# Other slots for a tail's events, a last tail in halves, and transfers asked for a stage sooner

## The reference

```python
theta = 2*pi*freq[ids]*t + phase[ids]
h = concat(amp[ids]*sin(theta), amp[ids]*cos(theta)) @ W_proj + b_proj + bias[ids]
x = layernorm(h)
Q, K, V = split(x @ W.T + b, 16 heads of 32)
S = K Q.T * scale + decay, causal           # softmax over S, times V
h = h + (softmax(S) @ V) @ o_w.T + o_b
x = layernorm(h)
score = sqrt(softplus(x @ gate_w.T))        # 32 experts
top6 of score + bias; weight = score / sum(score of top6) * 1.5
routed = sum over top6 (at most 192 rows an expert, in the order of the rows):
         weight * (silu(x @ w_gate) * (x @ w_up)) @ w_down
shared = clip(silu(x @ sg.T) * (x @ su.T), -10, 10) @ sd.T
out = h + routed + shared
```

## Time and profile before

| | before |
|---|---|
| median of 3 runs | 3718.28 us (3714.33 to 3722.51) |
| the profiled execution, its time | 3716.85 us |
| its span | 3715.1 us |
| TensorE busy, mean granted clock | 3207.5 us (86%), 0.935 |
| VectorE, ScalarE, GpSimd busy | 2157.7, 1201.6, 1756.5 us |
| embed, to | 261 us |
| attend, steps | 305 to 3224 us |
| last tail | 3224 to 3386 us |
| experts | 3386 to 3715 us |

### The profile page before, as it was taken

One profiled execution on the slowest core, in us unless ns is written; L12 is line 12 of the kernel. 1 busy time (PEld: TensorE's weight loads), 2 busy tenths in 40 slices (PEclk: granted clock), 3 DMA queues, 4 the chain that ended last, 5 costly groups with the idle time before them and its releaser, 6 DMA issues. The chain is left out here.

```text
span 3715.1 us, 61950 instructions
## 1 busy us (share of the span) xinstructions
PE 3207.5 (86%) x20352; PEld 1660.1 (45%) x20360; DVE 2157.7 (58%) x6046; ACT 1201.6 (32%) x2745; POOL 1756.5 (47%) x988
## 2 busy tenths in 40 slices
PE   4657999999899989999999898999999998675998
PEld 2333444444444444444444444444444443344775
DVE  6843444566656665666566656665666566663554
ACT  3651333233323332333333333333333333211111
POOL 5730454555555555555455545554555455622333
PEclk8878999999999999999999999999999998787999
DMA  5762300121111001100110011001100100005996
GB/s 189 254 258 84 100 30 12 35 74 57 59 59 50 23 24 36 37 22 22 38 35 23 21 39 35 22 23 38 35 21 25 37 15 21 29 15 166 258 257 151
DMA packets 121805, 253.61 MB, mean 68 GB/s; under 512 B 38748, under 2 KB 39388, under 8 KB 118928
## 3 DMA queue, kind: packets, MB, share of 16 engines
q1 hardware_dynamic: 76720, 197.22, 16.0%
q0 software_dynamic: 44048, 49.26, 5.2%
q10 hardware_dynamic: 720, 3.15, 0.2%
HBM read 144.61 MB, written 202.16 MB: 93 GB/s over the span
## 5 line engine op out<-in xcount | busy, mean ns | idle before, releaser
L855 POOL TENSOR_TENSOR a_first_probs<-a_first_probs,a_probs 128x2048 f32<-128x2048 f32 (+3 forms) x320 | 1030.6, 3221 | 1130.5 <-ACT a_probs L941 1038.7
L1084 DVE CUSTOM_DVE_ANT_0 a_unused<-a_ps_ring,a_decay 128x512 bf16<-128x512 f32 (+3 forms) x1536 | 778.6, 555 | 957.5 <-PE a_ps_ring L1374 952.0
L941 ACT ACTIVATE a_probs<-a_ps_ring 128x512 f32<-128x512 f32 (+3 forms) x1280 | 505.0, 472 | 461.1 <-PE a_ps_ring L1408 286.8
L1398 PE MATMUL a_ps_ring<-a_k_t,a_q_t 32*128 32x512 f32 (+3 forms) x3072 | 412.0, 538 | 66.6 <-DVE a_row_max L1084 44.4
L866 POOL DMA_INDIRECT d_slots<-a_rows,a_place_i x373 | 379.2, 1017 | 134.4 <-issue 71.6
L1374 PE MATMUL a_ps_ring<-a_q_t,a_k_t 32*128 32x512 f32 (+3 forms) x3072 | 396.5, 540 | 17.9 <-DVE a_row_max L1084 12.5
L1472 PE MATMUL a_ps_dense<-a_sd,a_inner_t 128*128 128x512 f32 x224 | 158.8, 848 | 147.4 <-DVE a_gate_up L1203 147.4
L941 ACT ACTIVATE a_first_probs<-a_ps_ring 128x512 f32<-128x512 f32 x256 | 135.7, 605 | 415.3 <-PE a_ps_ring L1408 392.3
L1398 PEld LDWEIGHTS a_ps_ring<-a_k_t,a_q_t 32*128 32x128 f32 x3072 | 144.8, 185 | 267.6 <-issue 147.9
L1421 PE MATMUL a_ps_heads<-a_probs,a_values 128*32 128x512 f32 (+3 forms) x2560 | 263.3, 484 | 0.0
L1362 PE MATMUL a_ps_dense<-a_normed_t,a_q_w 128*128 128x512 f32 x512 | 240.5, 613 | 24.7 <-DMA a_normed_t<-d_normed_t 22.2
(11 more groups left out here) (226 smaller groups left out, 4372.7 us busy)
## 6 DMA issues: line engine op xcount, KB each, us to landing
d_hidden<-e_hidden SPq DMA_DIRECT2D x8, 2048.0 KB
d_normed_t<-e_normed_t SPq DMA_DIRECT2D x8, 2048.0 KB
x_w_gate<-w_gate SPq DMA_DIRECT2D x32, 512.0 KB, 6.3
x_w_up<-w_up SPq DMA_DIRECT2D x32, 512.0 KB, 7.6
x_w_down<-w_down SPq DMA_DIRECT2D x32, 512.0 KB
a_normed_t<-d_normed_t SPq DMA_DIRECT2D x7, 2048.0 KB, 7.8
a_residual<-d_hidden SPq DMA_DIRECT2D x56, 256.0 KB, 2.7
d_hidden<-a_residual SPq DMA_DIRECT2D x56, 256.0 KB, 2.0
```

The source lines that it names most:

```text
L855: nc.gpsimd.tensor_tensor(total_of, total_of, probs_of(m)[:, :, 0:width], ALU.add).then_inc(added, 1)
L941: nc.scalar.activation(probs_of(m)[:, h, 0:width], score_bank(m, h)[:, 0:width], ACT.Exp).then_inc(exp_done, 1)
L1084: nc.vector.tensor_tensor_reduce(unused[:, (HG * k + h) % N_UNUSED, 0:width], row_bank(k, h)[:, 0:width], decay[:, at:at + width], 1.0, NE ...
L1398: nc.tensor.matmul(score_bank(m, h)[:, 0:width], q_t[st.g][dims, j * P:(j + 1) * P], k_t[st.g][dims, i0:i0 + width], start=True, stop=False)
```

## The change

1. **Slots.** Other entries in the tables.
2. **Last tail in halves.** Four tiles at once instead of two, in an order of 37 dense uses written out by hand, with six banks. `Part` holds the small tiles of a half, `late_parts` both; `find_late_places` is `find_places` for four tiles. Small operations on VectorE work on four tiles each; the shared expert still goes by quarters of two tiles (`late_inner`, `late_gate_up`). GpSimd multiplies the last heads ahead of the 12 scatters of the last step, and then issues 48.
3. **Shared tiles.** The q, k, v weights and the normed rows have tiles that live through all blocks (`Shared`). SP loads the weights in batch 2 of embed, and batch 0's rows between the stores of batch 6 and those of batch 7. The weights of experts 0 and 1 go to the same tiles (3 MB), issued by SP at the start of the last step, with the last batch's hidden rows; `load` leaves them out for these two. To make room, embed keeps its waves in the tile of its sines (so the sines of batch b wait until TensorE has turned the waves of b - 1), and some of its constants lie in the shared tiles.

```diff
-PROJECT_AT = {0: ((2, A), (3, A), (3, C), (4, C), (7, C), (9, C)),
-              1: ((0, C), (1, C), (2, C), (3, C), (7, C), (9, C)),
-              2: ((1, C), (2, C), (3, C), (4, C), (7, C), (9, C)),
-              3: ((0, C), (1, C), (2, C), (3, C), (7, C), (9, C))}
-OUT_AT = ((0, A), (0, C), (1, C), (2, C), (6, A), (7, A), (8, A), (9, A))
+PROJECT_AT = {0: ((2, C), (3, B), (3, C), (4, B), (7, C), (9, C)),
+              1: ((0, B), (1, C), (2, C), (3, C), (7, C), (9, C)),
+              2: ((1, C), (2, C), (3, C), (4, B), (7, C), (9, C)),
+              3: ((0, B), (1, C), (2, C), (3, C), (7, C), (9, C))}
+OUT_AT = ((0, A), (0, C), (1, C), (2, B), (6, B), (7, A), (8, A), (9, A))
-QUARTER_AT = {True: ((4, A), (4, B), (5, C), (6, C), (8, C), (10, C), (11, A), (11, C)),
-              False: ((4, A), (4, B), (5, C), (6, C), (8, C), (10, C), (11, A), (11, C))}
-STATS_AT = {True: (2, 1), False: (1, 1)}
-NORMALISE_AT = {True: (3, 1), False: (3, 1)}
-SOFT_SUM_AT = {True: (6, 1), False: (6, 1)}
+QUARTER_AT = {True: ((4, A), (4, C), (5, C), (6, C), (8, C), (11, A), (11, B), (11, C)),
+              False: ((4, A), (4, C), (5, C), (6, C), (8, C), (11, B), (11, B), (11, C))}
+STATS_AT = {True: (2, 1), False: (0, 1)}
+NORMALISE_AT = {True: (3, 1), False: (1, 1)}
+SOFT_SUM_AT = {True: (7, 1), False: (6, 1)}
-COUNT_AT = {True: (9, 1), False: (9, 1)}
+COUNT_AT = {True: (10, 0), False: (10, 0)}
-RSTD_AT = {True: 3, False: 2}
+RSTD_AT = {True: 3, False: 1}
-ROOT_AT = {True: 7, False: 7}
-LATE_SUMS_AT, LATE_MAXIMA_AT, EARLY_SUMS_AT, EARLY_MAXIMA_AT = (1, A), (1, B), (5, A), (5, B)
+ROOT_AT = {True: 7, False: 8}
+LATE_SUMS_AT, LATE_MAXIMA_AT, EARLY_SUMS_AT, EARLY_MAXIMA_AT = (1, A), (2, A), (5, A), (5, B)
-LATE_INVERT, EARLY_INVERT = (1, 2, 3, 4), (6, 8, 9, 10)
-LATE_MULTIPLY, EARLY_MULTIPLY = 5, 11
+LATE_INVERT, EARLY_INVERT = (1, 1, 4, 4), (6, 8, 8, 9)
+LATE_MULTIPLY, EARLY_MULTIPLY = 5, 10
-LATE_BANKS = 4
+LATE_BANKS = 6
+LATE = [("sums", 1, None), ("out", 1, None), ("out", 0, None), ("out", 2, None), ("out", 3, None),
+        ("out", 4, None), ("out", 5, None), ("turn", 0, None), ("turn", 1, None), ("turn", 3, None),
+        ("turn", 2, None), ("out", 6, None), ("route", 0, None), ("out", 7, None), ("up", 0, 0),
+        ("turn", 4, None), ("turn", 5, None), ("turn", 7, None), ("up", 1, 0), ("place", 0, None),
+        ("turn", 6, None), ("route", 1, None), ("up", 0, 2), ("up", 0, 1), ("up", 1, 1),
...
# embed, SP
+                if b == 2:
+                    sp.wait_ge(v_b_turned, 1)
+                    for tile, name, arrived in zip(common.projections, "qkv", common.weights_in):
+                        sp.dma_start(tile[:], io[f"{name}_w"]).then_inc(arrived, 16)
+                if b == NB - 2:
+                    sp.wait_ge(hidden_done, NT * (NB - 2))
+                    sp.wait_ge(normed_out[0], 16 * (NB // 2 - 1))
+                    first = common.normed_t()
+                    sp.dma_start(first[:, :, 0:HALF], dram["normed_t"][0, :, :, 0:HALF]).then_inc(common.normed_half_in, 16)
+                    sp.dma_start(first[:, :, HALF:T], dram["normed_t"][0, :, :, HALF:T]).then_inc(common.normed_in, 16)
...
# embed, ACT
-                wait_from_1(act, waves_done, b)
+                wait_from_1(act, wave_ps_full, 2 * b)
...
# attend, SP, at the start of the last step
+                if st.g == G - 1 and not st.rows:
+                    sp.wait_ge(scores_full, ITEMS * (FINAL - 2))
+                    for i in range(NT):
+                        sp.dma_start(late_hidden[i], dram["hidden"][NB - 1, tile_rows(i), :]).then_inc(late_in, 16)
+                    for e, (w_gate, w_up, w_down) in enumerate(common.weights()):
+                        sp.dma_start(w_gate, io["w_gate"][e]).then_inc(common.up_in[e], 16)
+                        sp.dma_start(w_up, io["w_up"][e]).then_inc(common.up_in[e], 16)
+                        sp.dma_start(w_down, io["w_down"][e]).then_inc(common.down_in[e], 16)
...
# VectorE, last tail
+            late_stats(7, chain)
+            take_moments(late_parts[1], chain)
+            normalise_late(1, chain)
+            choose(LATE_X + 0, late_parts[0], chain)
+            count_chosen(late_parts[0], chain)
+            find_late_places(0, late_parts[0], late("place", 0), chain)
+            late_gate(0, 0, chain)
+            soft_parts(late_parts[1], late("route", 1), chain)
+            soft_sum(LATE_X + 1, late_parts[1], chain)
...
# experts, load
+                if known is not None and known < FIRST_EXPERTS:
+                    return
```

More of the change, by code:

```diff
@@ L456 @@
 FINAL = G * NB
+LATE_X = QUARTERS * (NB - 1)
 SHIFT = 5
@@ L1121, in take_stats, with take_moments @@
+            def take_moments(k, chain):
                 chain.wait_apart(passed)
-                for j in range(2):
-                    chain.done(nc.vector.bn_aggr(moments[:, j, :], stats[:, j, :]))
+                for j in range(k.n):
+                    chain.done(nc.vector.bn_aggr(k.moments[:, j, :], k.stats[:, j, :]))
                 chain.wait()
-                nc.vector.tensor_scalar(variance[:], moments[:, :, 1], EPS, None, ALU.add).then_inc(var_done, 1)
-            def normalise(x, into, tiles, chain):
+                nc.vector.tensor_scalar(k.variance, k.moments[:, :, 1], EPS, None, ALU.add).then_inc(var_done, 1)
@@ L1220, in find_places @@
-                chain.done(nc.vector.tensor_tensor(place[:], place[:], over[:], ALU.add))
-                chain.done(nc.vector.tensor_tensor(counts_b[:], counts_b[:], chosen_b[:, 0, :], ALU.add))
+                chain.done(nc.vector.tensor_copy(rows[p][:, :, D], token[:]))
+                chain.done(nc.vector.tensor_tensor(k.place, k.place, k.over, ALU.add))
+                chain.done(nc.vector.tensor_tensor(counts_b[:], counts_b[:], k.chosen_b[:, 0, :], ALU.add))
                 chain.wait()
@@ L1336, in _ @@
             for_batches(dve, step)
-            for i in range(2):
-                add_late(i, late("out", i))
-            norm = norm_chain(0)
-            take_late_stats(0, norm)
-            for piece in range(PIECES):
-                invert_sums(1, piece, late("sums", 1))
-            normalise_late(0, norm)
-            for q in range(QUARTERS):
-                quarter(q)
+            chain = Chain(dve, late_step, 0)
+            add_late(1, late("out", 1))
+            add_late(0, late("out", 0))
@@ new lines, in _ @@
+            invert_sums(1, 0, late("sums", 1))
+            invert_sums(1, 1, late("sums", 1))
+            late_stats(1, chain)
+            invert_sums(1, 2, late("sums", 1))
+            add_late(2, late("out", 2))
+            invert_sums(1, 3, late("sums", 1))
+            late_stats(0, chain)
+            add_late(3, late("out", 3))
+            late_stats(3, chain)
+            late_stats(2, chain)
+            take_moments(late_parts[0], chain)
+            normalise_late(0, chain)
+            add_late(5, late("out", 5))
@@ new lines, in _ @@
+            late_stats(5, chain)
+            add_late(4, late("out", 4))
+            late_stats(4, chain)
+            add_late(6, late("out", 6))
+            soft_parts(late_parts[0], late("route", 0), chain)
+            late_stats(6, chain)
+            soft_sum(LATE_X + 0, late_parts[0], chain)
+            add_late(7, late("out", 7))
+            late_stats(7, chain)
+            take_moments(late_parts[1], chain)
+            normalise_late(1, chain)
+            choose(LATE_X + 0, late_parts[0], chain)
@@ L1348, in _ @@
+            add_shared(late_hidden[7], late("down", 1, 3))
+            add_shared(late_hidden[4], late("down", 0, 2))
         @block.tensor
@@ L1546, in _, with experts @@
                     out_project(NB - 1, arg, use)
[L1547 to L1552 removed]
+                elif kind == "turn":
+                    turn(LATE_X + arg // 2, late_rows[arg // 2], arg % 2, use)
+                elif kind == "route":
+                    tiles = range(arg * HALF_TILES, (arg + 1) * HALF_TILES)
+                    for i in tiles:
+                        turned = late("turn", i)
+                        pe.wait_ge(turned.free, turned.n + 1)
+                    route([(late_rows_t[i // 2], i % 2) for i in tiles], use)
+                elif kind == "up":
+                    for j in range(2):
+                        turned = late("turn", 2 * q + j)
+                        pe.wait_ge(turned.free, turned.n + 1)
+                    up(late_rows_t[q], arg, use)
+                elif kind == "place":
+                    if arg > 0:
+                        pe.wait_ge(counts_summed, 1)
+                    count_earlier(LATE_X + arg, late_parts[arg], use)
+                else:
+                    down(LATE_X + q, late_inner[q], arg, use)
 DEEP = 4
[L1561 removed]
+def experts(nc, io, dram, common):
     with ExitStack() as ctx:
```

538 lines of the change are left out of this document (321 added, 217 removed).

## The result

The changed kernel takes 3670.41 us (median of 4 runs, 3667.42 to 3672.14), the kernel before 3716.8 (4 runs): a ratio of 0.987, interval 0.9855 to 0.9885. That is 46 us faster, where I had forecast 122, and outside my range.

A forecast was written before the change was run, and what follows sets the result against it. TensorE's waits in the attention loop, a chain over several engines in the late tail, and the two stage changes were taken as bounds: 3716.85 - 70 - 39 - 7 - 6 gave 3595 us, range 3560 to 3655.

The forecast's parts named there:

- Loop: Attention loop: new slots shorten TensorE's waits in 28 steps with a tail; 70 us gained, from 20 to 120.
- GpSimd's multiplication fits into its idle time in slot 10: Attention loop: moved from slot 11; with the add still holding gate 1's product, the chain ends 1.0 us earlier.
- two products: Attention loop: GpSimd operations of 1.28 us each, said to hold gate 1's first product on VectorE until both are through.
- The turns: Attention loop, turn 1 moved behind the row scores: 1.4 us each in second and fourth steps, 0.3 in the third.
- the 1.0: Attention loop, first step of a batch: outs and projections move and the wait for the residual goes, 1.0 us.
- the shorter chain: Attention loop, VectorE's inversion and gate before down 0: 1.0 us less, plus 0.5 filled by attention matmuls, 1.5 a step.
- 19 more: Attention loop: extra us if VectorE and GpSimd had no lock, the chain gaining 1.7 us, 0.7 more a step.
- the clock fell: Attention loop, down 0: a stall of about 3.8 us still lowers TensorE's clock, so 1.8 us a step stay.
- Rival 1: Attention loop: slots only shift the stall, down 0 waiting for place and its product as before; 3645 to 3665, chance 0.17.
- Late tail: Last batch's tail in halves: first scatter at + 56.4, last at + 116.9 instead of 156.2; 39 us gained (30 to 45).
- Start: Start of attention: rows and weights loaded early, 10.9 us less 3 and 1; 7 us gained (2 to 11).
- Experts: Start of experts: first two experts' weights already there, so the second turn follows at once; 6 us gained (4 to 7).

The follow-up runs named there:

- changed_again: The changed kernel, unaltered, run again on chip 5, which showed no pauses: 3640.4 us, ratio 0.9808 to the kernel before.
- before_again: The kernel before, unaltered, run again on chip 5 for a trace beside changed_again: 3709.7 us, ratio 0.9994.
- count_first_again: The kernel count_first, unaltered, run again on chip 11, which showed no pauses: 3604.9 us, ratio 0.9720 to the kernel before.
- gate_before_add: On count_first, a second wait: GpSimd's add of slot 11 also waits until gate 1 is through; 3581.3 us, ratio 0.9650 to the kernel before.
- count_first: On the changed kernel, one wait: GpSimd's slot 10 multiplication of the heads waits until VectorE has counted the chosen; 3641.8 us on chip 3, ratio 0.9793.
- multiply_11: The changed kernel with one table entry taken back, GpSimd's multiplication of the heads at slot 11 again: 3658.9 us, ratio 0.9837 to the kernel before.
- slots_alone: The kernel before with all slot tables of the changed kernel and nothing else: 3712.9 us, ratio 0.9982.

## Why the prediction was wrong

**Loop, wrong.** The step that failed: "GpSimd's multiplication fits into its idle time in slot 10". It fits for GpSimd, and I had seen that VectorE's product beside GpSimd's work is held (of the "two products" that I named there, the second, L855, is an add); but I asked only what the new slot does for the operation that had been held before, not which operation of VectorE now stands beside the moved one. It was the cast of the count, held 3.5 us in 20 of 28 steps while two operations of GpSimd follow each other without a gap. The starts of the softmax sums (mean of three batches) give the balance by part of a step:

| us gained | slots 5 to 0 | slots 1 to 5 |
|---|---|---|
| first step, then into the second | + 2.0 | + 1.5 |
| second step, into the third | - 1.1 | - 1.3 |
| third step, into the fourth | - 1.0 | + 1.5 |
| fourth step, into the first | - 1.5 | - 0.2 |
| sum, forecast | - 1.6, + 6.0 | + 1.5, + 4.1 |

The first step, in which the cast isn't held, gained 2.0 where I had forecast 1.5; the others lost. The turns gave 1.5 where I had put 1.4 in the second and fourth step. In the third I had put + 0.3: the projection in (4,B) waits 0.70 for ScalarE's copy of turn 0 as turn 1 did, another 0.62 goes to ScalarE's wait before the row maxima, and the sums run at the slow clock. The 0.62 isn't what made the loss: without pauses (changed_again beside before_again) this part still loses 1.5. The first gave nothing of the 1.0.

How good was the rest of the forecast? Only the cast was missing from it; the gate's product it had left held. That is count_first_again: its loop takes 2897.9 us, 53.9 less than that of before_again (2951.8), where I had forecast 70. So with the cast freed the shorter chain and the turns gave three quarters. With both waits (gate_before_add) it takes 2874.0, 77.8 less; the prediction's own figures for that are 70 and 19 more. Of the 16 us that lack with the cast freed, the third and first steps' parts above (forecast + 0.3 and + 1.0 a batch) are the larger share; why the third loses 1.2 to 1.5 stays open in part. And the clock fell all the same, as I had assumed: down 0 still takes 3.8 us in 24 of 28 steps of gate_before_add.

Rival 1 (3645 to 3665) came nearest, but it named another mechanism: not the product of place, but the cast and the row maxima behind it.

The Trainium skill ("SBUF — State Buffer", Who interferes with whom) has an exclusive lock between VectorE and GpSimd, and the trace agrees: the cast ends as GpSimd's pair does, and takes 0.20 once GpSimd starts later. I had used that rule for one product only; read against each new neighbour it would have put the cast on the list.

**Late tail, mis-sized on one chip.** First scatter at + 55.6 (forecast 56.4); the last at + 128.4 instead of 116.9, with the pauses. Without them it is + 115.2. The trace that I forecast from wasn't free of them: the kernel before takes 156.2 us here in it and 150.5 in before_again, so on a chip without pauses the gain is 35 and not 39.

**Start, right.** The stores ended 2.2 us later, where I had taken off 3 for the rows and 1 for the rest; gained 8.7 of 10.9. The rule that all issuing engines share the 16 DMA engines (the Trainium skill, "DMA: Bandwidth & Descriptors", Issuing engines are not separate DMA queues) would have cost up to 6.5 us; from the issue of the last store to the end of the stores it is 1.5 us more than before (12.1 beside 10.6).

**Experts, right.** 5.6 us to the first `up`, 0.9 behind it; forecast 6.

**The sum.** 122 were forecast: the loop is 64 us short, the late tail 11. On a chip without pauses the changed kernel gains 69; there the loop is 53 us short, and 37 of them come back with count_first's one wait (2934.5 to 2897.9).

## What to carry to other kernels

When an operation of GpSimd is moved, list what VectorE does beside it in the new place, and in the order in which both engines really arrive there: an idle gap of the one engine is no free place for the other. Two operations of GpSimd in a row can hold VectorE for both (here in 20 of 21 steps); where the slack is GpSimd's, a semaphore wait on GpSimd is cheap, and here two of them gave 59 us on top of the change. And look at the waits of the engine that sets the end by name before and after: a wait that gets shorter (147 to 81 us over the run) proves nothing while another (44 to 90) grows.

## What the runs showed that I had not expected

Two programs ran unaltered in two places: the changed kernel took 3670 and 3640 us, count_first 3642 (chip 3) and 3605 (chip 11), while the kernel before moved by only 7 to 13 (3717 and 3723 beside 3710). In the slower traces ScalarE waits for 1.1 us before it takes the row maxima, 18 times in the first trace, for a release that comes 1.6 us after the records of TensorE's matmuls end; in the late tail ScalarE stands 22.5 us (4.9 in changed_again), VectorE 18.1 (0.5), and TensorE starts an instruction, matmul or weight load, each 0.7 us. The first trace of the changed kernel, count_first and multiply_11 show both, slots_alone the first; no trace from chips 5, 11 and 15 shows either. Common to both is that TensorE, or its release, is late. I don't know the cause, and no record of the trace tells it.

GpSimd's work doesn't slow every operation of VectorE: beside its adds the row maxima (L1084 in the kernel before, L1192 in the changed one) keep their 0.55 us and the reciprocals (L1207) their 0.95, while the cast and the products of two operands in SBUF are held until GpSimd ends.
